# Products that nothing reads ahead of the causal stage's strips and in its first steps, and an earlier first release

## The chip, the core and the metric

The kernel runs on one core of a Trainium2 chip. The time is the device time of one execution in microseconds. The core has four compute engines that run their own instruction streams and meet at semaphores: TensorE (PE, matrix products, with its weight loads shown as PEld), VectorE (DVE), ScalarE (ACT) and GpSimd (POOL). SyncE (SP) issues most of the transfers.

## The reference

Four layers follow one another on x of shape (4, 512, 128), each with a residual and a layer norm:

```python
x = _layernorm(x + _L0_attn_ref(x, ...))   # retention: 16 heads, q k^T times a decay mask, normed, silu gate, Wo
x = _layernorm(x + _L0_ffn_ref(x, ...))    # two layers: windowed attention (8 heads of 64, window 64) and a gated GELU layer
x = _layernorm(x + _L1_attn_ref(x, ...))   # causal attention: 16 heads of 8, q and k layer-normed per head
x = _layernorm(x + _L1_ffn_ref(x, ...))    # ternary weights: silu(x w1) * (x w2), GELU h1, GELU h2, w3
```

The third is the one that the change touches. Inside it:

```python
q, k, v = (x @ W.T for each); k = _layernorm(k, ...); q = _layernorm(q, ...)      # over the 8 values of a head
dot = einsum('bihd,bjhd->bhij', q, k) * scale; dot = where(causal, -inf, dot)
out = einsum('bhij,bjhd->bihd', softmax(dot), v) @ Wo.T + bo
```

## The kernel before, in words

A loop of two iterations takes two batches each, here called a pair; a pair has 8 tiles of 128 tokens. In each iteration every engine runs `retention`, twice `window_layer` and `gelu_layer`, then `causal` and `mlp`. The order of the work is written out by hand, engine by engine, and semaphores tie the engines together. All f32 products of TensorE show in the trace as two instructions each.

Start and release. Each engine begins an iteration with `pair_begin`, which waits until the semaphore `go` has been raised once for each iteration so far. For the first iteration SyncE raises it: it issues six transfers (the first cut of the constants, both halves of x, the masks, rows and a cut of the weights), waits for the second half of x, for the first weights and for the second cut of the constants (the last two are issued by ScalarE), issues five more transfers (L1841 to L1846) and then raises `xi_free` and `go`. The second iteration's `go` follows the end of the first. Before its own `pair_begin` VectorE centres some weights (`centre_values`, L1328 to L1332), and GpSimd copies a mask and waits for rows. In `retention` TensorE transposes x (`features`, L384) as soon as x has come (`x_first`), ScalarE copies the result out (L1356), TensorE projects (`projected`, L414), and VectorE scales the projections (L931).

The causal stage. TensorE makes q, k and v of the first four tiles (`project`, L659), then `narrowed(1, 1)` (L629), the last products of the layer before. Meanwhile VectorE computes the norms of q and k (L1168 to L1193, with Newton steps in `roots`) and writes the parts of the strips (L1203, L1204). `q_strips(0)` and `k_strips(0)` wait for the semaphore `strips_ready`, transpose four blocks each (L384), and ScalarE copies them out (L1356). Then come the steps s = 0 to END - 1. A unit u is four heads of one batch; it takes three steps (NG = 3), and there are eight units. In a step TensorE runs:

- `first_pass`: two fills of scores for the maxima (L709), then the causal mask added by products (L696); VectorE reduces them to maxima (`maxima`, L1212), and after three steps negates them (`negated`)
- at some steps `features3` and `shifted_strips` (transposes of the strips with the negated maxima in them)
- `second_pass`, four steps behind (LAG = 4): scores again, transposed (L728); ScalarE takes the exponential (L1554), GpSimd clears what lies above the diagonal (`keep`, L1787)
- `values` (L742), `q_strips`, `head_outputs`, `k_strips` and `project` at the steps that the tables name; VectorE divides the head outputs (`weighted`, L1233)

At steps 2 to 5 VectorE also squares and sums the norms of the tiles 4 to 7 (L1168), and at step 5 it runs `roots` once more.

Banks. PSUM has eight banks of 512 columns. The fills of both passes go round the bank pairs 0-1, 2-3 and 4-5; a fill waits for the maxima or the exponential of the fill that had the pair before. Bank 7 holds the values' sums, bank 6 serves transposes. `take` gives out a bank and makes TensorE wait until the bank's last content has been read.

Of the kernel before, what the change touches and what calls it, by code (L numbers as in the profile page):

```python
# [21 lines left out]
P = 128  # L22
# [43 lines left out]
def build(nc, x, wts, rows, consts, out):  # L66
    with ExitStack() as ctx:
# [3 lines left out]
        def sem(name):  # L71
            return ctx.enter_context(nc.semaphore(name))
# [33 lines left out]
        def w_(name):  # L106
            a, n = WEIGHTS[name]
            return W[:, a:a + n]
# [98 lines left out]
        go = sem("go")  # L207
# [62 lines left out]
        def take(pe, key, until, bank=None):  # L270

            if bank is None:
                bank = turn[0] % 7
                turn[0] += 1
            for s, v in last[bank] or []:
                pe.wait_ge(s, v)
            last[bank] = until
            place[key] = bank
            return psum[bank]
# [30 lines left out]
        def fills_a(s):  # L310
            return (2 * s, 2 * s + 1) if s < STEPS else ()
# [10 lines left out]
        OUT_AT = {NG * u + LAG + NG: u for u in range(G)}  # L322
        HEADS_AT = {NG * u + LAG + NG + 1: u for u in range(G)}
        WEIGHTED_AT = HEADS_AT
        FEATURES3_AT = 1
        PROJECT_AT = {1: 4, 2: 5, 3: 6, 4: 7}
        STATS_AT = {2: 4, 3: 5, 4: 6, 5: 7}
# [53 lines left out]
        def _(pe):  # L381
# [237 lines left out]
            def narrowed(l, b):  # L619

                pe.wait_ge(hh_ready, 3 * (2 * l + b) + 3)
                for t in range(NT):
                    n = G * l + NT * b + t
                    at = t * P if side_by_side(l, b) else 0
                    if t == 0 or not side_by_side(l, b):
                        bank = take(pe, ("w2", n), [(xf_ready, n + NT if side_by_side(l, b) else n + 1)],
                                    bank=NARROW[l, b][t])
                    for kb, K in enumerate(KB):
                        mm = pe.matmul(bank[:, at:at + P], hh2[0:K, b, kb, t * P:(t + 1) * P],  # L629
                                       w_(f"w2_{l}")[0:K, kb * P:(kb + 1) * P], start=(kb == 0), stop=(kb == 2))  # L630
                    mm.then_inc(pe_w2, 1)
# [21 lines left out]
            def causal():  # L653
# [18 lines left out]
                def q_strips(u):  # L672
                    pe.wait_ge(strips_ready, NT * (u // 4 + 1))
                    bank = take(pe, ("qS", u), [(qS_ready, u + 1)], bank=6)
                    transposes(bank, strip_sources(QS, u)).then_inc(pe_qS, 1)
# [6 lines left out]
                def shifted_strips(u):  # L682
                    pe.wait_ge(negmax_ready, u + 1)
                    bank = take(pe, ("qS2", u), [(qS2_ready, u + 1)], bank=6)
                    transposes(bank, strip_sources(QS, u)).then_inc(pe_qS2, 1)

                def next_pair(key, until):
                    i = filled[0] % 3
                    filled[0] += 1
                    for n in range(2):  # L690
                        take(pe, (key, n), until, bank=2 * i + n)
                    place[key] = i
                    return i
# [83 lines left out]
                for g in range(NT):  # L777
                    project(g, g)
                narrowed(1, 1)
                q_strips(0)  # L780
                k_strips(0)
                for s in range(END):
                    first_pass(fills_a(s))
                    if s == FEATURES3_AT:
                        features3(1)
                    if s in Q2_AT:
                        shifted_strips(Q2_AT[s])
                    second_pass(fills_b(s))
                    if s in V_AT:
                        values(*V_AT[s])  # L790
                    if s == FINISH_AT:
                        finish_first()
                    if s in Q_AT:
                        q_strips(Q_AT[s])
                    if s in HEADS_AT:
                        head_outputs(HEADS_AT[s])
                    if s in K_AT:
                        k_strips(K_AT[s])
                    if s in PROJECT_AT:
                        pe.wait_ge(xT_ready, 4)  # L800
                        project(PROJECT_AT[s], 7)
                    if s == GATHER_AT:
                        gather(0)
                    if s == FEATURES4_AT:
                        pe.wait_ge(loaded[4], 16)
                        features(4, 0, xM_ready, 2 * G + NT, bank=6)
                    for k in HIDDEN_AT.get(s, ()):
                        i = filled[0] % 3
                        filled[0] += 1
                        hidden(0, k, (2 * i, 2 * i + 1))  # L810
# [1017 lines left out]

        @block.sync
        def _(sp):  # L1830
            sp.dma_start(C[:, 0:CONST_CUTS[1]], consts[:, 0:CONST_CUTS[1]]).then_inc(consts_loaded[0], 16)
            for b in range(2):
                sp.dma_start(x_in[:, 4 * b:4 * b + 4, :], x[b].rearrange("(t p) d -> p t d", p=P)).then_inc(x_first[b], 16)
            sp.dma_start(arena[:, STAGING:STAGING + MASKS_WIDTH], consts[:, CONSTS_WIDTH:]).then_inc(masks_loaded, 16)
            sp.dma_start(R[:, 0:ROW_CUTS[1]], rows[:, 0:ROW_CUTS[1]].to_broadcast([P, ROW_CUTS[1]]))\
                .then_inc(rows_loaded[0], 16)
            sp.dma_start(W[:, WEIGHT_CUTS[1]:WEIGHT_CUTS[2]], wts[:, WEIGHT_CUTS[1]:WEIGHT_CUTS[2]]).then_inc(loaded[1], 16)
            sp.wait_ge(x_first[1], 16)
            sp.wait_ge(loaded[0], 16)
            sp.wait_ge(consts_loaded[1], 16)  # L1840
            sp.dma_start(C[:, CONST_CUTS[2]:CONST_CUTS[3]], consts[:, CONST_CUTS[2]:CONST_CUTS[3]])\  # L1841
                .then_inc(consts_loaded[2], 16)
            sp.dma_start(R[:, ROW_CUTS[1]:], rows[:, ROW_CUTS[1]:].to_broadcast([P, ROWS_WIDTH - ROW_CUTS[1]]))\
                .then_inc(rows_loaded[1], 16)
            for i in range(2, 5):
                sp.dma_start(W[:, WEIGHT_CUTS[i]:WEIGHT_CUTS[i + 1]], wts[:, WEIGHT_CUTS[i]:WEIGHT_CUTS[i + 1]])\  # L1846
                    .then_inc(loaded[i], 16)
            sp.sem_inc(xi_free)
            sp.sem_inc(go)
            with sp.Fori(0, 2) as it:  # L1850
                sp.wait_ge(pads_ready, 1)
                for l in range(2):
                    for g in range(G):
                        n = G * l + g
                        sp.wait_ge(vA_ready, n + 1)
                        if n >= 4:
                            sp.wait_ge(pe_O, 2 * (n - 3))
                        sp.dma_start(vS2[64:P, n % 4, :, :], vA2[0:64, n % 4, :, :]).then_inc(vS_landed[n % 4], 16)
                        if g % NT < NT - 1:
                            if n >= 3:  # L1860
                                sp.wait_ge(pe_O, 2 * (n - 2))
                            sp.dma_start(vS2[0:64, (n + 1) % 4, :, :], vA2[64:P, n % 4, :, :])\
                                .then_inc(vS_landed[(n + 1) % 4], 16)

                sp.wait_ge(pe_h2, 1)
                sp.wait_ge(h1_ready, 1)
                sp.wait_ge(h0_ready, 5)
                sp.wait_ge(rstd_ready, LN3 + G)
                for s in cleared[EARLY]:
                    sp.sem_clear(s)  # L1870
                for b in range(2):
                    sp.dma_start(x_in[:, 4 * b:4 * b + 4, :], x[2 + b].rearrange("(t p) d -> p t d", p=P))\
                        .then_inc(x_first[b], 16)
                for g in range(G):
                    b, t = divmod(g, NT)
                    if g == NT:
                        for s in cleared[BETWEEN]:
                            sp.sem_clear(s)
                    sp.wait_ge(out_ready, g + 1)
                    sp.dma_start(out[2 * it + b].rearrange("(t p) d -> p t d", p=P)[:, t, :], xi[:, g, :])\  # L1880
                        .then_inc(stored, 16)
                    if g == NT:
                        for s in cleared[RESULTS]:
                            sp.sem_clear(s)
                sp.wait_ge(arrived, 4 * (it + 1))
                sp.sem_inc(settle)
                for s in cleared[ENDING]:
                    sp.sem_clear(s)
                sp.drain().then_inc(go, 1)
                sp.wait_ge(stored, 16 * G)  # L1890
                sp.sem_clear(stored)
                sp.sem_inc(xi_free)
            for b in range(2):
                sp.wait_ge(x_first[b], 16)
# [108 lines left out]
```

## Time and profile before

| what | us |
|---|---|
| median of 3 timed runs | 1041.69 (1039.55 to 1044.32) |
| the profiled execution | 1053.3 |
| its span, first to last instruction | 1051.6 |
| TensorE busy in the span | 879.2 |
| VectorE busy | 662.8 |
| ScalarE busy | 491.4 |
| GpSimd busy | 477.9 |

Times in the views are microseconds from the span's start. An engine is busy while an instruction runs; in brackets stands how long it had been idle before, and what ended that. The granted clock of TensorE is given as a share of 2.4 GHz: 1.00 is 2.4 GHz, 0.50 is 1.2 GHz.

### The profile page before, as it was taken

The numbers are of one execution on the slowest core, as the hardware profiler recorded it, in microseconds if no ns is written. First come the engines' busy times: TensorE is split into PE (matmuls) and PEld (weight loads), VectorE is DVE, ScalarE is ACT, GpSimd is POOL, SyncE is SP. The second block draws the span as 40 slices with busy tenths as digits, with TensorE's granted clock in tenths as the row PEclk, the third lists the DMA queues.
The fourth block names the chain that finished last, engine by engine and source line by source line (L and its number), as shares of the span: only waits on it lengthen the run. The fifth ranks groups of instructions, "written<-read, shape, count | busy, mean of one in ns | idle before, by whom it ended". The sixth has DMA issues, their size and how long they took to land.

```text
span 1051.6 us, 19025 instructions
## 1 busy us (share of the span) xinstructions
PE 879.2 (84%) x6808; PEld 540.4 (51%) x6808; DVE 662.8 (63%) x1690; ACT 491.4 (47%) x1010; POOL 477.9 (45%) x501
## 2 busy tenths in 40 slices
PE   5876998889875788899987669988998587888998
PEld 2553676457643344444545536764676344444445
DVE  3897795569678655430168887946795776653302
ACT  2213775367634555542141147744775344655321
POOL 2666883188532422310056678823885324222101
PEclk9999999999996889899989999999999866998999
DMA  9100010011000000000000010100110000000000
GB/s 356 57 1 22 21 28 6 11 26 33 7 1 1 1 2 1 2 1 21 11 13 2 2 32 17 27 2 21 27 28 1 1 1 1 2 1 1 1 20 21
DMA packets 11636, 21.67 MB, mean 21 GB/s; under 512 B 1424, under 2 KB 6928, under 8 KB 11024
## 3 DMA queue, kind: packets, MB, share of 16 engines
q1 hardware_dynamic: 11248, 18.60, 6.0%
q10 hardware_dynamic: 288, 1.78, 0.4%
q8 instruction: 58, 0.95, 0.4%
q14 instruction: 42, 0.34, 0.1%
HBM read 11.87 MB, written 1.05 MB: 12 GB/s over the span
## 4 chain that ended last, share of the span: by engine, by line
PE 53%; DVE 28%; POOL 8%; issue 5%; ACT 4%; DMA 1%; SPq 0%; POOLq 0%; DVEq 0%; ACTq 0%
PE bank L831 11%; PE bank L384 9%; DVE arena L1212 4%; PE bank L742 4%; PE bank L639 3%; PE bank L821 3%; DVE arena L1060 3%; PE bank L709 2%; DVE arena L895 2%; PE bank L728 2%; POOL arena L1722 2%; POOL arena L1730 2%; DVE arena L953 2%; DVE arena L1071 2%; PE bank L414 2%
## 5 line engine op out<-in xcount | busy, mean ns | idle before, releaser
L384 PE MATMUL bank<-consts_sb,arena 128*128 128x128 f32 x1040 | 166.8, 304 | 98.7 <-DVE arena L903 24.3
L384 PEld LDWEIGHTS bank<-consts_sb,arena 128*128 128x128 f32 x1040 | 129.7, 155 | 165.8 <-issue 79.9
L1356 ACT ACTIVATE arena<-bank 128x512 f32<-128x512 f32 (+2 forms) x300 | 147.5, 556 | 143.2 <-PE bank L384 84.8
L1642 POOL TENSOR_TENSOR rstd<-vareps,neghalf 128x1 f32<-128x1 f32 x96 | 53.0, 553 | 250.2 <-DVE vareps L890 248.8
L1212 DVE TENSOR_REDUCE arena<-bank 128x2 f32<-128x1024 f32 (+3 forms) x128 | 98.0, 819 | 47.7 <-PE bank L696 47.0
L1722 POOL TENSOR_TENSOR arena<-arena,neghalf 128x16 f32<-128x16 f32 x32 | 93.1, 2908 | 64.5 <-DVE arena L1062 64.5
L1787 POOL TENSOR_SCALAR_AFFINE_SELECT arena<-arena 128x256 f32<-128x256 f32 x128 | 51.2, 413 | 141.7 <-ACT arena L1554 139.0
L831 PE MATMUL bank<-arena,weights 128*128 128x512 f32 x256 | 111.9, 594 | 1.6 <-ACT arena L1610 1.6
L503 PE MATMUL bank<-weights,x_features 128*128 128x512 f32 x192 | 98.8, 629 | 15.1 <-DVE arena L1075 9.2
L1554 ACT ACTIVATE arena<-bank 128x1024 f32<-128x1024 f32 (+1 forms) x96 | 81.6, 881 | 29.0 <-PE bank L728 28.6
L1474 ACT ACTIVATE arena<-bank,arena 128x128 f32<-128x128 f32 x256 | 69.7, 384 | 50.9 <-DVE arena L1103 50.9
L831 PEld LDWEIGHTS bank<-arena,weights 128*128 128x128 f32 x256 | 48.0, 190 | 61.0 <-issue 57.4
L1730 POOL TENSOR_TENSOR arena<-arena 128x512 f32<-128x512 f32 x56 | 71.1, 1270 | 2.2
L1610 ACT ACTIVATE arena<-bank,weights 128x512 f32<-128x512 f32 x32 | 22.0, 688 | 99.4 <-PE bank L831 99.4
L728 PE MATMUL bank<-q_strips_shifted,k_strips 32*128 32x512 f32 (+3 forms) x256 | 46.0, 423 | 26.7 <-DVE arena L1212 26.4
L1735 POOL TENSOR_TENSOR arena<-arena 128x512 f32<-128x512 f32 x56 | 58.5, 1044 | 4.4
L888 DVE BATCH_NORM_STATS2 bn<-bank 128x6 f32<-128x128 f32 x16 | 4.7, 294 | 87.4 <-PE bank L845 87.4
L1103 DVE TENSOR_REDUCE arena<-bank 128x4 f32<-128x512 f32 x64 | 41.1, 686 | 28.6 <-PE bank L579 28.3
L742 PE MATMUL bank<-arena 128*32 128x256 f32 (+3 forms) x512 | 54.3, 526 | 5.2 <-POOL arena L1787 3.3
L503 PEld LDWEIGHTS bank<-weights,x_features 128*128 128x128 f32 x192 | 33.1, 197 | 40.0 <-issue 15.7
L1423 ACT ACTIVATE arena<-bank 128x512 f32<-128x512 f32 x64 | 37.8, 612 | 26.8 <-PE bank L503 26.0
L1691 POOL TENSOR_TENSOR arena<-arena,neghalf 128x16 f32<-128x16 f32 x16 | 48.4, 3023 | 2.5 <-DVE arena L992 2.5
(172 smaller groups left out, 1643.7 us busy)
## 6 DMA issues: line engine op xcount, KB each, us to landing
arena<-arena SPq DMA_DIRECT2D x56, 130.0 KB, 2.3
weights<-wts_dram SPq DMA_DIRECT2D x1, 2824.0 KB, 19.1
weights<-wts_dram SPq DMA_DIRECT2D x1, 1817.0 KB, 13.1
weights<-wts_dram SPq DMA_DIRECT2D x1, 1561.0 KB, 9.2
arena<-x_dram SPq DMA_DIRECT2D x6, 256.0 KB, 3.2
consts_sb<-consts_dram ACTq DMA_DIRECT2D x1, 1226.5 KB, 7.4
out_dram<-x_inner SPq DMA_DIRECT2D x16, 64.0 KB, 1.5
consts_sb<-consts_dram SPq DMA_DIRECT2D x1, 768.0 KB, 4.5
```

The lines of the kernel that those rows point to most:

```text
L384: mm = pe.transpose(bank[:, i * P:(i + 1) * P], src, ident)
L503: pe.matmul(bank[:], hT[:, b, t * P:(t + 1) * P], w_(f"qkv2_{l}")[:, 512 * j:512 * j + 512], start=True, stop=True).then_inc(done, 1)
L728: mm = pe.matmul(psum[2 * i + n][:, at:at + (NT - t) * P], kS[rows, u % 3, t * P:(t + 1) * P], qS2[rows, u % 2, t * P:S], start=(at == 0), ...
L742: mm = pe.matmul(psum[7][32 * h:32 * h + 32, t * P:S], vp[:, 4 * b + t, 4 * quad + h, :], PT3[group][:, h, at:at + (NT - t) * P], start=(t ...
L831: mm = pe.matmul(bank[:], w_(name)[:, 512 * c + k * P:512 * c + (k + 1) * P], src[:, b, c, :], start=(c == 0), stop=(c == 3))
L1212: ins = dve.tensor_reduce(mx3[:, u % 2, t, 2 * p:2 * p + 2], scores[:, :, at:at + (t + 1) * P], AX, ALU.max)
L1356: return act.activation(dst, src, ACT.Copy)
L1474: ins = act.activation(sm2[:, g % 2, h, :], held(("S", n, c))[:, m * P:(m + 1) * P], ACT.Exp, bias=a2["nb"][:, 4 * c + m:4 * c + m + 1], s ...
L1554: act.activation(PT3[group][:, 2 * p:2 * p + 2, 0:wide], pair_view(place["B", f])[:, :, 0:wide], ACT.Exp).then_inc(E_ready, 1)
L1722: pool.tensor_tensor(rn2[:, g % 2, :], ss2[:, g % 2, :], neghalf[:].to_broadcast([P, 16]), ALU.pow).then_inc(rn_ready, 1)
L1730: pool.tensor_tensor(straight2[:, at], straight2[:, at], swapped2[:, at], ALU.add)\
L1735: pool.tensor_tensor(qk2[:, g % 2, at].rearrange("p (h d) -> p h d", d=D2), straight2[:, at].rearrange("p (h d) -> p h d", d=D2), rn2[:, g ...
```

## The change

Three edits. TensorE gets a helper, `idle_products`, that takes bank 6 and multiplies a block of the weights already in SBUF by 512 of their columns, n times over, each product starting the bank afresh; nothing reads the result. It is called once with n = 12 between `narrowed(1, 1)` and `q_strips(0)`, and once with n = 1 behind `first_pass` in each of the steps 0 to 8. SyncE raises `go` ahead of its first transfer, no longer behind its last.

```diff
+        IDLE_PRODUCTS, IDLE_AT = 12, {s: 1 for s in range(9)}
...
+                def idle_products(key, n):
+                    bank = take(pe, ("idle", key), [], bank=6)
+                    for _ in range(n):
+                        pe.matmul(bank[:], w_("vg1")[:, 0:P], w_("vg1"), start=True, stop=True)
+
...
                 narrowed(1, 1)
+                idle_products("strips", IDLE_PRODUCTS)
                 q_strips(0)
                 k_strips(0)
                 for s in range(END):
                     first_pass(fills_a(s))
+                    if s in IDLE_AT:
+                        idle_products(s, IDLE_AT[s])
                     if s == FEATURES3_AT:
                         features3(1)
...
         def _(sp):
+            sp.sem_inc(go)
             sp.dma_start(C[:, 0:CONST_CUTS[1]], consts[:, 0:CONST_CUTS[1]]).then_inc(consts_loaded[0], 16)
...
             sp.sem_inc(xi_free)
-            sp.sem_inc(go)
             with sp.Fori(0, 2) as it:
```

## Rows read from the trace of the kernel before

**Rows 1.** The page: TensorE's granted clock in 40 slices of the span, in tenths.

```profile
PEclk9999999999996889899989999999999866998999
```

**Rows 2.** Busy by stretch: length, PE, PEld, DVE, ACT, POOL, granted clock, DMA, GB/s.

```profile
315.90:332.90 17.00, 8.00 (x43) 6.14 (x44) 14.35 (x40) 5.46 (x20) 7.63 (x9) 0.50 0.00 0
...
350.10:356.80 6.70, 4.67 (x35) 2.55 (x36) 3.61 (x6) 1.74 (x6) 3.11 (x5) 0.50 0.00 0
374.00:384.10 10.10, 9.91 (x53) 5.09 (x54) 4.06 (x11) 4.48 (x6) 2.35 (x6) 0.50 0.01 2
438.80:530.80 92.00, 86.10 (x316) 43.94 (x312) 19.75 (x64) 28.35 (x39) 11.01 (x21) 1.00 0.04 12
834.80:858.50 23.70, 14.73 (x68) 9.30 (x68) 18.32 (x48) 8.06 (x27) 7.60 (x9) 0.50 0.00 1
872.30:889.20 16.90, 15.40 (x90) 7.71 (x91) 9.07 (x21) 9.34 (x24) 8.94 (x16) 0.50 0.00 1
```

**Rows 3.** Timeline of the start (start, duration, instructions); the landing time of x's two transfers.

```profile
1.28 0.98 SPq L1833 DMA_DIRECT2D arena<-x_dram  x2
...
DMA to landing us min/median/max: 7.6/7.8/8.0
...
12.45 1.28 ACT L1356 ACT_TABLE_LOAD   x1 [12.45 <-SPq L1849]
...
12.48 1.94 PE L384 MATMUL bank<-consts_sb,arena 128*128 128x128 f32 x8 [12.48 <-SPq L1849]
12.49 0.43 DVE L1332 TENSOR_TENSOR rowconsts<-rowconsts,arena 128x256 f32<-128x256 f32 x1
...
13.74 1.32 ACT L1356 ACTIVATE x_features<-bank 128x512 f32<-128x512 f32 x2
...
14.49 5.87 PE L414 MATMUL bank<-x_features,weights 128*128 128x512 f32 x8
...
16.68 0.75 DVE L931 SCALAR_TENSOR_TENSOR arena<-bank,weights,consts_sb 128x512 f32<-128x512 f32 x1 [3.12 <-PE bank L414]
```

**Rows 4.** Timeline: wide products at full clock, and TensorE around the first strips.

```profile
20.20 3.60 PE L422 MATMUL bank<-weights,x_features 128*128 128x512 f32 x8
...
309.50 2.84 PE L629 MATMUL bank<-weights,arena 128*128 128x128 f32 x24
...
323.39 1.11 PE L384 MATMUL bank<-consts_sb,arena 128*128 128x128 f32 x4 [11.05 <-DVE arena L1204]
```

**Rows 5.** Timeline of the first pair's steps 0 to 9: VectorE's maxima, TensorE's waits.

```profile
328.53 2.35 DVE L1212 TENSOR_REDUCE arena<-bank 128x2 f32<-128x1024 f32 x2
...
334.86 1.29 DVE L1212 TENSOR_REDUCE arena<-bank 128x2 f32<-128x512 f32 x2 [0.99 <-PE bank L696]
...
338.16 0.63 PE L384 MATMUL bank<-consts_sb,arena 128*128 128x128 f32 x4 [0.78 <-ACT q_strips_shifted L1356]
...
344.19 1.29 DVE L1212 TENSOR_REDUCE arena<-bank 128x2 f32<-128x512 f32 x2 [0.79 <-PE bank L696]
...
352.13 0.58 PE L728 MATMUL bank<-q_strips_shifted,k_strips 32*128 32x256 f32 x2 [4.08 <-DVE arena L1212]
...
357.02 2.48 DVE L1212 TENSOR_REDUCE arena<-bank 128x2 f32<-128x256 f32 x4 [3.24 <-PE bank L696]
...
364.13 1.94 PE L742 MATMUL bank<-arena 128*32 128x512 f32 x8 [2.09 <-POOL arena L1787]
...
367.15 0.26 DVE L1233 RECIPROCAL arena<-bank 128x16 f32<-128x16 f32 x1 [2.82 <-PE bank L384]
```

**Rows 6.** Timelines: step 13's maxima in both pairs, and the second pair's strips and L1233.

```profile
387.76 0.42 DVE L1212 TENSOR_REDUCE arena<-bank 128x2 f32<-128x256 f32 x1 [1.85 <-PE bank L696]
...
842.26 1.11 PE L384 MATMUL bank<-consts_sb,arena 128*128 128x128 f32 x4 [11.05 <-DVE arena L1204]
...
888.20 0.26 DVE L1233 RECIPROCAL arena<-bank 128x16 f32<-128x16 f32 x1 [2.04 <-PE bank L384]
...
905.69 0.42 DVE L1212 TENSOR_REDUCE arena<-bank 128x2 f32<-128x256 f32 x1 [1.86 <-PE bank L696]
```

## The prediction

> **What bounds the kernel now.** I read the page first. TensorE is by far the busiest engine, and the row of granted clocks is lowest in slice 13 and again in slices 33 and 34 of 40 (6 tenths in each) [rows 1]. A busy engine at half its clock is the first thing to look for. The reader should find that both low stretches lie where the causal stage of a pair of batches begins. The busy times by stretch then put numbers on it [rows 2]. In the first pair the clock is 0.50 of full (1.2 GHz) from 315.9 to 332.9 us, at 0.50 again from 350.1 to 356.8 and from 374.0 to 384.1. The second pair has two low stretches, 834.8 to 858.5 and 872.3 to 889.2. Between 438.8 and 530.8, where wide products of the same type follow one another, the clock is 1.00 throughout. What TensorE did before the first fall is in the timeline [rows 4]: its last products before the strips begin at 309.50 and take 2.84 us, and then it stands idle for 11.05 us, until the strips are ready at 323.39. In the second pair the same wait is there, 518.9 us later.
>
> The second thing is the start. The timeline of the first 20 us [rows 3] shows TensorE and ScalarE both released by SyncE's L1849 at 12.45 us. By then SyncE has waited for the inputs and issued five more transfers. The first half of x was issued at 1.28 and needed 7.6 us, the second about 0.5 us later and needed 8.0: they are in SBUF at 8.9 and 9.7.
>
> **The change part by part.**
> *The release.* `go` is raised ahead of SyncE's first transfer instead of behind its last. What it is moved past is SyncE's queue alone: eleven DMA issues and three waits, none of which changes place, so nothing in the queue waits for more than one increment (about 0.1 us). TensorE then starts when the first half of x is in SBUF, at 8.9, and no longer at 12.48. Its eight transposes cost 1.94 us, so the first four end at 9.9; the second four wait for 9.7 and end near 10.9. ScalarE's table load of 1.28 us, which stood between 12.45 and 13.74, now runs while the inputs travel, and its copy (half of 1.32 us) ends at 10.6. The first projection (L414), at 14.49 now, can start at 11.0: 3.5 us earlier. VectorE is next in line: it finishes centring at 12.49 + 0.43 = 12.92 us either way, and the first product's result comes at 11.0 + 2.2 = 13.2 (2.2 us being the time from L414's start to VectorE's first use of it), so it is late by nothing. Projections, scores and states follow dynamically; the remaining weights were needed much later. The first pair alone gains this. Bounds: a gain of 4.5 if TensorE need not wait for the second four, and 1.7 if the clock's rise does not come forward with the work, because then 3.5 us more of it runs at 1.2 GHz. I take 3.5.
>
> *Twelve products ahead of the strips.* Each is 128x512 in f32, which the trace shows as two instructions; eight of them, L422, take 3.60 us at full clock [rows 4], so a product costs 0.86 to 0.9 us and twelve cost 10.3 to 10.8. They fit into the idle 11.05 us, with 0.3 to 0.7 us to spare, and bank 6 is free. They cost nothing as long as the clock stays at 1.00 under them, and the dense stretch from 438.8 says that it does. Ahead of the strips nothing else waits behind them. If they end late there is more cover: VectorE takes up the first maxima at 328.53 without a wait in front of them, straight from its normalisations [rows 5]. At full clock two sets of transposes (1.11 us each at 323.39, 0.63 at 338.16) and the first scores are ready some 1.5 us earlier than now, and VectorE is not. So the first maxima do not move at all: this part of the gain is lost.
>
> *One product in each of steps 0 to 8.* 9 x 0.86 = 7.7 us of TensorE for each pair, directly behind the step's scores. What is queued behind each are the step's strips and the second pass, so the softmax waits for it, and the next step's maxima too. `take` also makes each wait for bank 6, that is, for ScalarE's last copy of a strip; TensorE waits for that copy in the same or the next step anyway, so I put it at nothing (bounds 0 and 0.3 us for a step). I walk the steps with the durations at full clock and compare VectorE's maxima:
>  - Step 2, at 334.86 now after 0.99 us idle: between the first maxima and the end of the low stretch TensorE has about four groups of transposes, scores and masks, each some 0.4 us shorter at full clock (0.48 for transposes). That is 1.5 us, one product of 0.86 stands in it, and 0.6 is gained: 334.3.
>  - Steps 3 to 5: the clock had already recovered here, so the products only cost. Three come before step 5's maxima (steps 2 to 4), 2.6 us, of which TensorE's waits for VectorE and ScalarE, such as the 0.78 before 338.16, absorb about half. The gain of 0.6 is used up first. Step 5's maxima go from 344.19 to 344.9: 0.7 us late, and the Newton roots on VectorE behind them pass it on.
>  - Step 6 has TensorE idle for 4.08 us before 352.13, waiting for the roots. The products of steps 5 and 6 go into it for nothing and the idle time shrinks to 2.7 us. TensorE goes on at 352.8, 0.7 late, but at full clock: what took 4.89 us (352.13 to 357.02) takes 2.9. Step 7's maxima come at 355.75, a gain of 1.3.
>  - L1233, at 367.15, waits for TensorE's values (1.94 us from 364.13) and transposes (1.1 us at this clock). At full clock the two take some 1.7 and not 3.05 us, and they begin 1.2 us earlier with step 7: 364.65. A gain of 2.5 for the first pair; 1.2 if the clock is low at this place as it is now.
> The second pair runs the same work 518.87 us later (its strips start at 842.26 where the first pair's start at 323.39). Its L1233, at 888.20, is 2.2 us behind that [rows 6], because its first low stretch lasted to 858.5. The walk removes that as well: 2.5 + 2.2, say 4.6.
>
> *The sum.* 3.5 + 2.5 + 4.6 = 10.6 us. The profiled execution is 1053.3 us (its span 1051.6 and 1.7 around it), so 1042.7 for it. It was 11.6 us longer than the median of the timed runs, 1041.69; I take the difference over: 1031.1.
>
> One rule of the Trainium skill speaks against the effort: "TensorE: Matmul & The Clock Gate", "What's actually happening", says that the penalty of the warm-up is under 1% of a typical kernel. The rows here disagree: the five low stretches alone are 74.4 us, 7% of the span. By the rule the products would be worth less than the release.
>
> **The rivals.**
> *A. The clock stays full behind step 8 too.* After L1233 the first pair needs 20.6 us to step 13's maxima at 387.76, with the low stretch from 374.0 in it; the second pair, with hardly any of it behind 889.2, needs 905.69 - 888.20 = 17.5 [rows 2, 6]. That is 3.1 us more: 1028.0. Against it: no product stands there.
> *B. The clock falls inside the steps all the same.* The wait of 2.7 us left in step 6 is the place; a low stretch there costs about what the second pair's longer one cost, 2.2 us a pair. 10.6 - 4.4 = 6.2: 1035.5. The skill's same page, "A second HAM failure mode: psum-queue depth-cycling", says that short idle times between groups of products, bank by bank, are enough to make the clock swing; that is this rival, and the low stretch from 374.0, with TensorE busy 9.91 of 10.1 us in it and small waits before it, agrees.
> *C. Slower: the clock falls under the twelve.* At 1.2 GHz they take 12 x 1.72 = 20.6 us instead of 10.3. The strips would start up to 9.5 us late; 1.5 us of that is covered by VectorE's normalisations, so 8 a pair: -3.5 + 16 = +12.5, 1054.2. It turns to a loss for the stage once they end about 2.2 us after 322.7. Only the rows from 438.8 to 530.8 speak against it, and strongly.
> *D. The products buy nothing.* If the timed executions, 11.6 us shorter than the profiled one, have little of the low clock, then the steps pay 0.7 us a pair and only the release is left: -3.5 + 1.4 = -2.1, 1039.6. The same time comes out if VectorE sets the pace after all. That the instructions are not issued I leave out, for nothing in the code could drop them.
>
> **How the numbers follow.** Forecast 0.43, A 0.17, B 0.22, C 0.06, D 0.12. A measurement of this kernel tells 0.5%, 5.2 us, from no change: 1036.5 and 1046.9. Forecast, A and about half of B lie below: 0.72. The rest of B, nearly all of D: 0.21. C and a little of D: 0.07. The range leaves out C and the far part of A: 1026 to 1040, which takes in the bounds of the release (1.7 to 4.5) at either end.
>
> **What the profile would show.** Right: L414 starts near 11.0 us and ScalarE's table load before 3; 24 matmul instructions between the last of L629 and the strips, 0.43 us each, with clock 1.00 and TensorE idle under 1 us before the strips; the first maxima after the strips' start by 5.1 us as before; L1233 about 41.3 us after the strips' start where it was 43.8 and 45.9 after it. Wrong: a clock of 0.50 under the twelve, strips later than 16 us behind the last L629, a low clock in steps 3 to 8, or matmuls of the steps that delay the maxima by more than 0.9 us each.

## The result, and the profile after

The change makes the kernel faster, but by less than I had forecast: the ratio of its runs to those of the kernel before is 0.993, with a 95% interval of 0.990 to 0.996 (20 runs of each). The medians of these 20 are 1038.58 us after and 1049.27 before; the median of 1041.69, from which the forecast was counted, was that of the first three of the 20. A second set of 12 runs on another chip gave 0.994 (0.991 to 0.997). The ratios here and below leave out the executions that are more than 1.5% above the fastest of their kernel (2 of the 20 before, 4 of the 90 in the table below, 1 of e12). The profiled execution is 1041.2 us, its span 1039.5.

Three views of the kernel after carry the reading. The start, from its timeline:

```profile
1.97 1.28 ACT L1366 ACT_TABLE_LOAD   x1 [1.97 <-DVEq L1349]
...
8.85 2.01 PE L386 MATMUL bank<-consts_sb,arena 128*128 128x128 f32 x8 [8.85 <-DMA arena<-x_dram]
...
10.74 5.04 PE L416 MATMUL bank<-x_features,weights 128*128 128x512 f32 x8
```

Against [rows 3] the table load has moved from 12.45 to 1.97, the transposes from 12.48 to the landing of x at 8.85, and the first projection (L416, that is L414 before) from 14.49 to 10.74. The causal stage of the first pair, from the timeline of TensorE and VectorE (the products that nothing reads are L692; L716 and L735 are the first and second pass, L1222 the maxima, L1243 the first head outputs):

```profile
304.27 10.46 PE L692 MATMUL bank<-weights 128*128 128x512 f32 x24
315.50 0.66 PE L386 MATMUL bank<-consts_sb,arena 128*128 128x128 f32 x4 [0.77 <-DVE arena L1214]
...
337.25 0.69 DVE L1222 TENSOR_REDUCE arena<-bank 128x2 f32<-128x512 f32 x1 [0.76 <-PE bank L703]
...
345.36 0.58 PE L735 MATMUL bank<-q_strips_shifted,k_strips 32*128 32x256 f32 x2 [2.67 <-DVE arena L1222]
...
358.87 0.26 DVE L1243 RECIPROCAL arena<-bank 128x16 f32<-128x16 f32 x1 [1.09 <-PE bank L386]
```

The busy times by stretch (length; busy time of PE, PEld, DVE, ACT, POOL with instructions; granted clock, DMA share, GB/s):

```profile
304.50:315.40 10.90, 10.24 (x24) 4.18 (x22) 9.28 (x26) 3.41 (x16) 3.28 (x4) 1.00 0.00 0
344.70:351.30 6.60, 5.94 (x39) 3.42 (x40) 3.33 (x6) 2.78 (x10) 3.69 (x6) 0.50 0.00 0
...
832.80:836.00 3.20, 3.09 (x11) 1.54 (x12) 2.63 (x10) 0.01 (x1) 1.74 (x3) 0.50 0.00 0
836.20:859.90 23.70, 19.80 (x134) 10.27 (x132) 19.41 (x44) 12.82 (x25) 3.96 (x7) 1.00 0.00 1
860.10:863.30 3.20, 3.20 (x22) 1.43 (x22) 1.50 (x3) 0.60 (x1) 1.87 (x3) 0.50 0.02 5
880.60:894.10 13.50, 13.50 (x82) 6.81 (x80) 5.25 (x10) 5.65 (x8) 3.03 (x8) 0.50 0.00 1
```

What the reader is to see: the twelve take 10.46 us at full clock, and of the 11.05 us of idle time in [rows 4] 0.77 are left. In the first pair the clock holds from there into the steps, through the place where it was low for 17 us [rows 2]. In the second it falls for some 3 us right behind the strips (832.8, the strips start at 830.11); the maxima behind that come as in the first pair all the same. Then, with the 2.67 us wait of step 6, it falls in both pairs, at about 344.6 and 860, and in the second pair once more at 880.

All times below of maxima and head outputs are counted from the start of the first strips of their pair. They compare kernels whose earlier stages drifted apart: from one execution to the next the causal stage of the first pair begins several microseconds earlier or later, with low stretches of the clock in the stages before it.

### The profile page after: what moved, and what is told of

Read it like the earlier page. It is cut to its first block, busy times and chain, and to the rows that moved or that the text cites. A ratio compares the mean times of both kernels' runs of the same rounds, so it can differ in the third digit from the quotient of the medians.

```text
span 1039.5 us, 19177 instructions
## 1 busy us (share of the span) xinstructions
PE 895.5 (86%) x6892; PEld 542.4 (52%) x6892; DVE 662.5 (64%) x1690; ACT 489.9 (47%) x1010; POOL 477.2 (46%) x501
## 4 chain that ended last, share of the span: by engine, by line
PE 52%; DVE 29%; POOL 8%; issue 5%; ACT 4%; DMA 1%; SPq 0%; POOLq 0%; DVEq 0%; ACTq 0%
PE bank L841 11%; PE bank L386 8%; DVE arena L1222 4%; PE bank L749 4%; PE bank L641 3%; PE bank L831 3%; DVE arena L1070 3%; DVE arena L963 2%; DVE arena L905 2%; PE bank L735 2%; POOL arena L1732 2%; PE bank L716 2%; POOL arena L1740 2%; DVE arena L1081 2%; PE bank L505 2%
## 5 line engine op out<-in xcount | busy, mean ns | idle before, releaser
L386 PE MATMUL bank<-consts_sb,arena 128*128 128x128 f32 x1040 | 159.6, 295 | 76.9 <-DVE arena L913 25.3
L386 PEld LDWEIGHTS bank<-consts_sb,arena 128*128 128x128 f32 x1040 | 124.5, 150 | 146.2 <-issue 66.9
L1222 DVE TENSOR_REDUCE arena<-bank 128x2 f32<-128x1024 f32 (+3 forms) x128 | 97.9, 818 | 46.2 <-PE bank L703 45.2
L735 PE MATMUL bank<-q_strips_shifted,k_strips 32*128 32x384 f32 (+3 forms) x256 | 42.4, 414 | 19.3 <-DVE arena L1222 19.1
L749 PE MATMUL bank<-arena 128*32 128x256 f32 (+3 forms) x512 | 51.9, 507 | 5.1 <-POOL arena L1797 3.3
## 6 DMA issues: line engine op xcount, KB each, us to landing
weights<-wts_dram SPq DMA_DIRECT2D x1, 1817.0 KB, 13.4
```

What stands on the lines that cost most here:

```text
L386: mm = pe.transpose(bank[:, i * P:(i + 1) * P], src, ident)
L735: mm = pe.matmul(psum[2 * i + n][:, at:at + (NT - t) * P], kS[rows, u % 3, t * P:(t + 1) * P], qS2[rows, u % 2, t * P:S], start=(at == 0), ...
L749: mm = pe.matmul(psum[7][32 * h:32 * h + 32, t * P:S], vp[:, 4 * b + t, 4 * quad + h, :], PT3[group][:, h, at:at + (NT - t) * P], start=(t ...
L1222: ins = dve.tensor_reduce(mx3[:, u % 2, t, 2 * p:2 * p + 2], scores[:, :, at:at + (t + 1) * P], AX, ALU.max)
```

## The experiments

The runs are named e1 to e12 in the table. For each kernel it has the mean time and the mean granted clock of its runs, the ratio to the kernel before with its interval, and the time that a line through its runs (time against granted clock) gives at a clock of 0.95. The line settled several questions: over the 90 runs of the kernel before that were made beside e1 to e12, the time falls by 7.0 us for each 0.01 of granted clock, and that kernel's line stands at 1031.3 us at 0.95. It has two limits. First, not every kernel reached 0.95: the highest clock of the kernel before, e1 and e12 is 0.942, the lowest of e7, e9 and e10 is 0.963. Their figures are the line drawn on, with a standard error of 0.4 us for the kernel before, 3 us for e1 and e10, 1.2 for e9 and 1.6 for e7; the others have 0.8 or less, e11 1.0. Second, the line gives every low stretch the same worth. 0.01 of some 1045 us is 20.9 us at half clock, so 7.0 us for that is a third of a us for each us of low clock, also where TensorE had nothing to do.

| kernel | runs | mean us | clock | ratio (95%) | us at 0.95 |
|---|---|---|---|---|---|
| before | 90 | 1045.1 | 0.930 | | 1031.3 |
| after | 20 | 1039.0 | 0.958 | 0.993 (0.990 to 0.996) | 1043.6 |
| after, again (e11) | 12 | 1036.9 | 0.962 | 0.994 (0.991 to 0.997) | 1044.3 |
| release only (e1) | 12 | 1044.3 | 0.927 | 1.000 (0.997 to 1.003) | 1028.1 |
| release only, again (e12) | 12 | 1042.0 | 0.929 | 0.999 (0.994 to 1.003) | 1028.2 |
| products only (e2) | 12 | 1043.9 | 0.955 | 0.999 (0.995 to 1.002) | 1047.0 |
| release, twelve (e3) | 12 | 1041.9 | 0.944 | 0.998 (0.994 to 1.001) | 1037.0 |
| release, twelve, four in step 6's wait (e4) | 12 | 1045.6 | 0.939 | 1.002 (0.999 to 1.005) | 1039.2 |
| release, nine (e5) | 14 | 1047.1 | 0.937 | 1.003 (1.001 to 1.006) | 1037.9 |
| after, two in each step (e6) | 12 | 1046.6 | 0.957 | 1.001 (0.997 to 1.005) | 1051.4 |
| after, seven in waits (e7) | 6 | 1031.0 | 0.973 | 0.987 (0.982 to 0.992) | 1046.5 |
| after, GpSimd later (e8) | 9 | 1036.2 | 0.962 | 0.992 (0.988 to 0.996) | 1043.4 |
| seven in waits, three in step 6's (e9) | 12 | 1031.4 | 0.975 | 0.989 (0.985 to 0.993) | 1048.4 |
| as e9, steps 2 to 8 empty (e10) | 6 | 1030.7 | 0.969 | 0.989 (0.984 to 0.995) | 1042.6 |

**The release alone.** The products are taken out, the release stays early.

```diff
-        IDLE_PRODUCTS, IDLE_AT = 12, {s: 1 for s in range(9)}
+        IDLE_PRODUCTS, IDLE_AT = 0, {}
...
-                idle_products("strips", IDLE_PRODUCTS)
```

> Only the early release; no product that nothing reads. Theory 1 (the release is worth its forward shift, and the clock's rise comes forward with it): the first projection starts near 10.7 us as in the changed kernel, 3.7 us earlier, and the time falls by 3.7 to 4.6 us, a ratio near 0.996. The first strips' wait stays 11 us, the clock falls in it, and the maxima of steps 5, 7 and the first head outputs lie 20.8, 33.6 and 43.8 us behind the strips as before. Rival (the products carry the whole gain): ratio 0.999 or above. Rival (the release carries the whole gain): ratio 0.993.

> The early release alone once more. Theory 1 (its 3.3 us are real, and the first measurement had runs with a lower clock, 0.927 against 0.929): at equal granted clock 3 to 3.5 us below the kernel before; ratio 0.996 to 0.998. Rival (the shift at the start is given back before the end): equal at equal clock, ratio 1.000.

Measured: 1.000 and 0.999, both intervals with 1 in them, and both above the ratios that I had expected. The first projection starts at 10.72 and 10.56 us, as in the changed kernel. At equal clock both stand 3.1 to 3.2 us below the kernel before (1028.1 and 1028.2 against 1031.3), and 3.2 and 3.7 at a clock of 0.93, which all three reached (1042.0 and 1041.5 against 1045.2). So the shift at the start is carried to the end; the rival that gives it back falls on the line, though the ratio by itself could not tell: the runs of either kernel come in clusters some 5 us apart, by the clock, and 3 us is less than one of these steps. In both kernels' two pairs step 5's maxima come at 21.6 to 21.7 us and the first head outputs at 44.4 to 44.5, one of them here (e12's, L1242), with the strips at 314.87:

```profile
359.28 0.26 DVE L1242 RECIPROCAL arena<-bank 128x16 f32<-128x16 f32 x1 [2.03 <-PE bank L386]
```

That is a result of its own: the two pairs in the profile of before, 43.8 and 45.9 us, lie to either side of what four others of the same work took.

**The products alone.** `go` is raised where it was.

```diff
-            sp.sem_inc(go)
             sp.dma_start(C[:, 0:CONST_CUTS[1]], consts[:, 0:CONST_CUTS[1]]).then_inc(consts_loaded[0], 16)
...
             sp.sem_inc(xi_free)
+            sp.sem_inc(go)
```

> The twelve and the nine products, the release as before. Theory 1: only what is left of the gain, 3 us, ratio near 0.997, because the steps give back what the full clock saves: maxima of step 5 at 21.7 us behind the strips, 0.9 us later than in the first pair of the kernel before. Rival (my forecast as it stands): 7.1 us, ratio 0.993, with the first head outputs 41.3 us behind the strips in both pairs.

Measured: 0.999 (0.995 to 1.002), which takes in theory 1's 0.997. Step 5 came at 21.7 in both pairs, as theory 1 had it; the first head outputs, which the rival has at 41.3 in both, came at 43.0 and 41.3. The granted clock rose from 0.929 to 0.955, which at 6.8 us per 0.01 would be worth 17.5 us; the mean fell by 1.4. At equal clock the kernel is 15.7 us slower than before (1047.0 against 1031.3). That is the finding of the case: the products buy clock, and it comes to almost nothing. The runs show where the 15.7 us go.

 - Some 5 us are no price at all. The clock that the twelve hold up in the idle 11 us helps nobody: 7.5 us were low there in each pair before, half of it of 1045 us is 0.007 of clock, 5 us on the line.
 - The nine in each pair cost 6.6 to 7.3 us: that is what the changed kernel has over e3, which lacks them, at equal clock (1043.6 and 1044.3 against 1037.0). It makes some 0.4 us for each of the 18, and e6 below gives 0.43. The traces say the same where they can be compared at full clock: 2.1 us up to step 5 in the first pair of e3, for the five products that lie before it.
 - The rest, about 4 us, is again clock that the line prices too high. e3 has the twelve alone and stands 8.8 us above the release alone, though its strips start 13.9 us behind the last L631, as without them. Its first pair has full clock where e1 has 12 us of low clock behind the strips. The line gives 4.0 us for that, an estimate, and the trace 2.1 (step 5 at 19.6 against 21.7), and there are two such stages in an execution.

**The twelve without the nine, and the wait of step 6 filled.** First no product in the steps; then, beside that, four ahead of the second fill of step 6's second pass, where TensorE waits for VectorE's roots.

```diff
-        IDLE_PRODUCTS, IDLE_AT = 12, {s: 1 for s in range(9)}
+        IDLE_PRODUCTS, IDLE_AT = 12, {}
...
+                        if f == 5:
+                            idle_products("hole", 4)
                         i = next_pair(("B", f), [(E_ready, f + 1)])
```

> Early release and the twelve products, none in the steps. Theory 1 (the step products cost what the clock gives back): the full clock lasts from the strips to about step 6; step 2 and step 5 maxima come at 10.4 and 19.6 us behind the strips instead of 11.2 and 21.7, but in the 4 to 5 us wait of step 6 the clock falls, so that the first head outputs lie about 42.5 behind them; ratio 0.992 to 0.993, as with the nine. Rival (the nine are needed to hold the clock): the clock falls already within steps 0 to 5, step 5 comes at 20.8 or later, ratio 0.996.

> Early release, the twelve products, none in the steps, but four products (3.5 us) inside the wait of step 6, ahead of the second fill of the second pass. Theory 1 (the fall behind step 6 comes from the wait there, and a full clock is worth 2 to 2.5 us from there to the first head outputs): the clock stays 1.00 through step 7, step 7 maxima come 31.5 to 32 us and the first head outputs 40.5 to 41 us behind the strips; ratio 0.989 to 0.990. Rival (the clock falls whatever stands in the wait): step 7 at 33.5 as in the kernel before, ratio 0.993.

In the first pair of each the theory holds. Without the nine, step 5's maxima come at 19.6 us, 2.1 earlier than with them. In e3 the clock falls in the wait of step 6, and the first head outputs come at 42.6. With the wait filled, in e4, the clock stays at full through it, and step 7 comes at 30.4 and the first head outputs at 39.0, earlier than I had expected. The row is e4's, with the strips at 319.91:

```profile
358.90 0.26 DVE L1245 RECIPROCAL arena<-bank 128x16 f32<-128x16 f32 x1 [1.09 <-PE bank L386]
```

In the second pairs it does not hold. There the clock fell within the first steps; stretches of e3 and of e4, with their strips at 837.76 and 828.16:

```profile
840.50:853.90 13.40, 12.78 (x60) 7.86 (x60) 9.62 (x23) 3.45 (x9) 3.49 (x3) 0.50 0.01 1
```

```profile
833.60:840.20 6.60, 5.55 (x26) 3.67 (x26) 4.52 (x6) 1.59 (x4) 2.20 (x1) 0.50 0.00 0
```

TensorE was busy 12.78 of 13.4 and 5.55 of 6.6 us in them, with small products. The rival is partly right: without the nine (e3, e4, and e10 below) the clock fell between the strips and step 6 in three stages of six, for 3 to 14 us; with the nine and the twelve it did so in one of 14, the second pair of after, for 3 us. Over the runs neither kernel differs from the kernel before by more than its interval, and the expectation of e4, 0.989, was missed by far.

**The nine without the twelve.**

```diff
-                idle_products("strips", IDLE_PRODUCTS)
```

> The changed kernel without the twelve; release early, one product in each of steps 0 to 8. Theory 1 (the twelve are hidden and hold the clock into the first steps; the nine alone start cold and cost 0.6 us each and more at the low clock): the clock falls in the 11 us wait, the first steps run low, step 5 maxima come 23 to 24 us behind the strips instead of 21.7; mean granted clock near 0.94; 3 to 5 us longer than the changed kernel, ratio to the kernel before 0.997 to 0.999. Rival (the nine alone bring the clock up within a step or two): as the changed kernel, 0.993.

Measured: 1.003 (1.001 to 1.006), slower than the kernel before, and 8 to 10 us slower than the changed kernel. The clock is at 0.50 from 307.5 to 324.4, the strips start in the middle of that, and products in the steps that run there cost double: step 5 at 23.4 us. Theory 1 had the mechanism and too small a price.

```profile
307.50:324.40 16.90, 7.05 (x30) 4.12 (x30) 13.63 (x39) 5.20 (x19) 7.87 (x9) 0.50 0.00 0
```

**Two products in each step.**

```diff
-        IDLE_PRODUCTS, IDLE_AT = 12, {s: 1 for s in range(9)}
+        IDLE_PRODUCTS, IDLE_AT = 12, {s: 2 for s in range(9)}
```

> The changed kernel with two products in place of one in each of steps 0 to 8; measures what a product there costs. Theory 1 (a step product is nearly all on the path to the maxima and costs 0.6 us or more): 18 more products, 11 to 15 us longer than the changed kernel, less at most 3 for a steadier clock; ratio to the kernel before 1.003 to 1.006; step 5 maxima 24.5 to 25.5 us behind the strips. Rival (TensorE's waits absorb them and the clock stays full): ratio 0.993 or below, step 5 at 22.

Measured: 1.001, 7.6 us more than the changed kernel by the means and 7.8 at equal clock (1051.4 against 1043.6), so 0.43 us for each of the 18 more. The rival falls. My price for the whole was too high: step 5 came at 24.8, 0.6 us for each of the five that lie before it, but the next maxima came 6.4 us behind these where the changed kernel has 6.7, and the clock did not fall in steps 0 to 8 here, in either pair.

**Products inside waits.** Beside all of the change, one product in each unit from the second on, ahead of the second fill of the second pass, where TensorE waits 0.82 us for the maxima; then also three in the wait of step 6; then that with the steps 2 to 8 left empty.

```diff
+                        if f % NF == 1 and u:
+                            idle_products(("wait", u), 1)
+                        if f == 5:
+                            idle_products("hole", 3)
                         i = next_pair(("B", f), [(E_ready, f + 1)])
```

> The changed kernel with one product more in each unit from the second on, put where TensorE waits 0.82 us for the maxima (ahead of the second fill of the second pass, group 0). Theory 1 (behind step 8 the low clock wanders through the later steps and costs 4 to 5 us a pair; a product inside a wait costs nothing): mean granted clock rises from 0.958 to about 0.97, the last head outputs come 120 to 122 us behind the strips in both pairs, ratio 0.988 to 0.990. Rival (the products lengthen the steps as much as the clock shortens them): ratio 0.993 to 0.997 at the higher clock.

> The changed kernel with the seven products inside the 0.82 us waits of units 1 to 7, and three more (2.6 us) inside the wait of step 6, ahead of the second fill of the second pass. Theory 1 (the fall that comes behind step 6 in both pairs is caused by the wait there and costs 2.1 us a pair): the clock stays 1.00 from the strips to the end of the steps, the first head outputs come 41.2 us behind the strips instead of 43.5, granted clock 0.98, time 1026 to 1028, ratio 0.983 to 0.985. Rival (the fall comes from the steps' small products, whatever stands in the wait): as the run with the seven alone, 0.987.

> As the run before it in this list, but one product in steps 0 and 1 only, not in steps 2 to 8. Theory 1 (a step product costs 0.4 to 0.6 us wherever TensorE has no wait behind it; once the clock is held otherwise it buys nothing): step 5 maxima 19.6 us behind the strips, head outputs 39 to 40, 2 to 3 us a pair faster, ratio 0.979 to 0.982. Rival (the nine are what holds the clock between the strips and step 6, as the second pairs of the two runs without them suggest, where it fell 2.6 and 5.3 us behind the strips): falls in steps 2 to 6, step 5 at 21 to 23, ratio 0.986 to 0.990.

The seven in the waits gave what they were expected to: 0.987 (0.982 to 0.992), clock 0.973, the last head outputs at 120.4 us in both pairs. The changed kernel (after) had 122.5 and 127.2 and 118.3 to 122.8 in the four stages of e8 and e11. What they take away is a low stretch of 10 us that begins 102 to 104 us behind the strips in four of those six stages. They are not quite free: at full clock a unit takes 11.65 us with one of them and 11.5 without, so 0.15 us for each of 0.87. The clock still fell behind step 6's wait in both pairs. The three products in that wait removed this fall in both, and the clock was full for 90 us of each causal stage. The rows are those 90 us of the first pair, the second has the same from 824.1 to 914.5, and what came behind them:

```profile
315.70:406.00 90.30, 80.68 (x634) 41.68 (x634) 61.57 (x135) 51.76 (x91) 27.24 (x55) 1.00 0.01 1
406.10:409.10 3.00, 3.00 (x14) 1.11 (x15) 1.39 (x7) 1.74 (x2) 1.87 (x5) 0.50 0.00 0
```

The first head outputs came at 41.8 us instead of 43.5. Together with e4 and e10 this shows the cause of the fall: with products in the wait (e4, e9, e10) the clock did not fall behind it in any of six stages, and with the wait left as it is, beside the nine (after, e2, e7, e8, e11), it fell in seven of ten. But the time did not follow: 0.989 (0.985 to 0.993), where I had expected 0.985 at most. The traces say why. About 90 us behind the strips the clock fell in both pairs for some 3 us, where e7 had none, and the unit there took 16.6 us against 15.0; the last head outputs came at 120.1 us, against 120.4 in e7. What was won behind step 6 was lost again at that place; why the clock fell there is open. In e10 step 5's maxima came at 20.5 and 21.7 us and the first head outputs at 40.5 and 42.3, with a fall of some 3 us in each pair, 39 and 18 us behind the strips; that is nearer to the rival, and the ratio of 0.979 to 0.982 was missed. At equal clock e10 stands 5.8 us below e9, but its figure is uncertain by 3 us, and the means of the two are 0.7 us apart. So once the waits are filled, the products of steps 2 to 8 neither help nor harm by anything that 6 and 12 runs can tell. All three beat both kernels; which of them is best is open.

**GpSimd later.** In the trace of after one small operation of VectorE's centring takes 1.98 us where it took 0.17. The edit makes GpSimd's first memsets wait until the centring is done.

```diff
             def retention():
+                pool.wait_ge(centred1, CENTRED1)
                 pool.memset(v1[:, :, :, V1 + 1:32], 0.0)
```

> The changed kernel, but GpSimd's first memsets wait until VectorE has centred its weights. Theory 1 (VectorE's 1.98 us for one small operation at 11.26 us, 0.17 before, comes from GpSimd's memsets that the early release moved beside it, and nothing waited for it): the operation takes 0.17 us again, centring ends near 12.9 instead of 14.7, the second group of products still starts near 15.6, time as the changed kernel, ratio 0.993. Rival (the slow operation held the start up): 1 to 2 us faster, 0.991.

The operation took 0.17 us again, the centring ended at 13.0 instead of 14.7, the second group of projections (L424) started at 15.33 instead of 15.63 (between 14.85 and 16.20 in the other kernels with the early release), and at equal clock the kernel stands where the changed one does (1043.4 against 1043.6). So the slow operation held up nothing that the times show. The profile of this kernel was worth more for its first causal stage, in which the clock happened to be full from the strips (318.37) for 100 us:

```profile
318.40:418.90 100.50, 82.58 (x714) 44.59 (x718) 71.80 (x160) 58.22 (x100) 32.05 (x66) 1.00 0.01 1
```

```profile
359.67 0.26 DVE L1243 RECIPROCAL arena<-bank 128x16 f32<-128x16 f32 x1 [1.08 <-PE bank L386]
```

The first head outputs come at 41.3 us, which is the time my walk gives for the changed kernel at full clock.

**The changed kernel again.**

> The changed kernel itself once more, on the chip and against the runs of the kernel before that the other runs of this call have. Theory 1: ratio 0.992 to 0.995, mean granted clock 0.956 to 0.960. Rival (its 20 runs were lucky, and the two parts, measured at 1.000 and 0.999, simply add up): ratio 0.997 to 0.999.

Measured: 0.994 (0.991 to 0.997), clock 0.962: theory 1. Its second pair had the full clock for 100 us behind the strips and reached 41.3 us again; its first fell at 344.3 and had 43.4. That the two parts measured alone (1.000 or 0.999, and 0.999) do not add up to 0.993 is open: at equal clock they do (-3.1 and +15.7 give 1043.9, measured 1043.6 and 1044.3), so the rest is a difference in the clock granted, 0.958 to 0.962 against 0.955, which is small and may be the luck of 12 runs.

## Why the prediction was right or wrong

**The release: right.** L414 was forecast at 11.0 and came at 10.74; the gain was forecast at 3.5 and is 3.1 to 3.3 at equal clock. The table load ran before 3.3 us. VectorE's centring was said not to be the later one, at 12.92 in any case. It ended at 14.70, because of GpSimd's memsets (e8), so that step's claim was wrong, and VectorE began at 15.17 and not at 13.2; TensorE's next group did not have to wait for more than that, which is why it cost nothing.

**The twelve: right.** 10.46 us against 10.3 to 10.8, clock 1.00 under them, 0.77 us idle before the strips, and the first maxima at 5.14 us behind the strips in every kernel, early clock or not.

**The steps up to 6: right in mechanism, near in size.** Step 2: 0.27 us earlier, 0.6 forecast. Step 5: 0.95 late against [rows 5], 0.7 forecast (against e1 and e12, which have the same work without products, it is 0.1 late). The wait of step 6: 2.67 us, 2.7 forecast.

**The step that failed is the one behind it.** The forecast let the clock stay full through that wait, and gave 0.22 to the case that it does not. Of eight causal stages in four profiles of this arrangement (after, e2, e8, e11) it fell there in five. Where it held, the first head outputs came at 41.3 us, as forecast, in three stages; where it fell, at 43.0 to 43.5. The price of the fall is 2.0 us a stage, 2.2 in the rival's sum; only its chance was wrong. The cause is the wait itself: with products in it there was no fall in six stages of three kernels.

**A term mis-sized by the reference.** I took the second pair's 45.9 us as what the change would have to beat and booked 4.6 us for it. Without products the stage takes 44.4 to 44.5 in all four stages of e1 and e12. So the gain of a stage up to the first head outputs is 1.2 us with the fall and 3.1 without, 1.9 on the mean of the eight, and 3.8 for both pairs where the forecast has 7.1. Of the 3.3 us that are missing the fall makes 2.5 (five eighths of 2.0, twice) and the reference 0.9. With the release's 3.2 the sum is 7.0 us; measured are 7.3 (0.7% of 1045), or 6.1 and 8.2 by the means of the two sets against that of the 90. That the sum comes so near is partly luck, for the products alone, e2, gained 1.4 us and not 3.8. One profile with two pairs that differ by 2.2 us should have told me how far apart two executions can be.

**The time itself.** 1031.1 us was forecast and 1038.6 measured, but only 3.3 us of the difference are the change (10.6 forecast, 7.3 measured). The start, 1041.69 us, was a median of three executions; the mean of the 20 is 1047.1, of the 90 others 1045.1.

**A comparison that does not hold.** I set 74.4 us of low clock, 7% of the span, against the under 1% of the Trainium skill ("TensorE: Matmul & The Clock Gate", "What's actually happening"). The 7% are the length of the stretches, not what they cost: by the line it is a third of that, 25 us or 2.4%, an estimate, and most of it comes in the middle of the kernel, not in a warm-up, of which the sentence speaks. In e2 the clock rose by 0.026, an estimated 54 us less of low clock, and the gain was 1.4 us. So the objection was nearer to the truth than I made it.

**The rivals.** B is what happened. The traces agree with the section of the Trainium skill that the prediction names for it ("TensorE: Matmul & The Clock Gate", "A second HAM failure mode: psum-queue depth-cycling") only in part: it speaks of frequent short idle times between groups of products, and what e4, e9 and e10 show is the effect of one wait, of 2.67 us beside the nine and about 4 without them. A came about in part and brought little: behind step 8 the clock stayed full to 80 us behind the strips in seven of the eight stages, but in e1 and e12, without products, it was full from 47 to 78 us as well, in all four. C did not occur. D had a true half: the products give back nearly all that they bring, partly by their own 0.4 to 0.6 us each in the steps, partly because the clock was worth less there than the line has it.

## What to carry to other kernels

A product that nothing reads is worth its place only where the engine waits anyway: in the 11 us before the strips it was free, in the waits of the later units it cost 0.15 us, behind each step's scores it cost half to two thirds of its length. Ask where the clock that it wins is worth something: in e2 0.026 more of clock, 17.5 us by the line, made the kernel 1.4 us faster, because much of it lay where TensorE had nothing to do or was not what the stage waited for. And take more than one profile of the kernel before when its own two halves differ.

## What the runs showed of the hardware

An operation of VectorE waited for GpSimd's memsets. In the kernel after, GpSimd's memsets begin at 11.08 us, and VectorE's operation on 16 columns, which began at 11.26, lasts until they are over:

```profile
10.80 0.42 DVE L1338 TENSOR_REDUCE arena<-weights 128x16 f32<-128x256 f32 x1 [9.76 <-DMA rowconsts<-rows_dram]
11.08 1.70 POOL L1673 MEMSET arena<- 128x1920 f32 x1 [0.84 <-DMA rowconsts<-rows_dram]
11.26 1.98 DVE L1340 TENSOR_SCALAR arena<-arena 128x16 f32<-128x16 f32 x1
12.71 0.50 POOL L1674 MEMSET arena<- 128x480 f32 x1
...
14.06 0.17 DVE L1340 TENSOR_SCALAR arena<-arena 128x16 f32<-128x16 f32 x1
```

With the memsets moved behind it the same operation takes 0.17 us:

```profile
11.37 0.17 DVE L1340 TENSOR_SCALAR arena<-arena 128x16 f32<-128x16 f32 x1
...
13.06 1.70 POOL L1674 MEMSET arena<- 128x1920 f32 x1 [2.70 <-DVE rowconsts L1342]
```

An operation with two tensors beside the same memset was not slowed: 0.43 us at 12.49 in [rows 3], where the memset began at 12.50, so the operation was the first of the two. The Trainium skill, "SBUF — State Buffer", "Who interferes with whom", says that a `tensor_scalar` of VectorE can use a pair of ports which it shares with GpSimd, that whoever starts first has it for the whole instruction, and that an operation with two inputs does not contend with a GpSimd instruction that only writes. Both rows agree as far as they go. That the operation also outlasted the second memset, which began 1.45 us behind it, does not follow from the section, and no run here tells why.

The granted clock can fall where no wait is longer than 1.5 us. Before the fall at 880.6 of after TensorE was busy 13.32 of 17.0 us, in the steps' small products, and its longest waits were 1.48, 0.82 and 0.71 us. In the low stretches behind a fall, such as 840.5 to 853.9 of e3 and from 880.6 of after, it was busy 95% and 100% of the time, and the clock stayed at 0.50. Yet in e8 it stayed at full from 357 to 418.9 us, through 62 us of the same steps without a product that nothing reads, with waits of up to 0.88 us. What tells these places apart was not tried.
